# Moving three waits and one load in a single-core adaLN block with attention and a mixture of experts

## The reference

```python
h = _layernorm(x) * (1 + ca) + sa
normed = h * rsqrt(mean(h * h) + EPS)
q, k, v = heads(normed @ W_qkv.T + b_qkv)
scores = where(causal_mask, -inf, q @ k.T)
attn = softmax(scores, axis=-2)                 # over the queries
x = x + ga * ((attn @ v) @ W_o.T + b_o)
h2 = _layernorm(x) * (1 + cb) + sb
score = softmax(h2 @ Wg + bg); idx = argmax(score); gate = max(score)
pos = (cumsum(onehot) - 1) at idx               # rank of the token in its expert
keep = pos < 256
y = relu(buf[e] @ W1[e] + b1[e]) @ W2[e] + b2[e]   # buf: kept rows, by expert and rank
x = x + gb * where(keep, y[idx, pos] * gate, 0)
```

## Time and profile before

| what | value |
|---|---|
| median of 3 runs | 1332.78 us (1331.36 to 1332.94) |
| profiled execution, its own time | 1330.97 us |
| its span, first to last instruction | 1329.2 us |
| mean granted clock of TensorE, share of full | 0.954 |
| PE busy | 1212.8 us (91%) |
| DVE, ACT, POOL busy | 857.6, 602.1, 342.0 us |
| chain that ended last | PE 76%, issue 9%, ACT 6%, DVE 6%, DMA 1%, POOL 1% |

### The profile page before, as it was taken

The page is one execution under the profiler, slowest core; times in us unless marked ns, Lnnn a source line. Parts: engine busy times, 40 slices in busy tenths (PEclk is TensorE's granted clock), DMA queues, the critical chain, the costliest instruction groups (busy, mean ns, idle before and its releaser), DMA issues.

```text
span 1329.2 us, 23812 instructions
## 1 busy us (share of the span) xinstructions
PE 1212.8 (91%) x7522; PEld 859.4 (65%) x7522; DVE 857.6 (65%) x2172; ACT 602.1 (45%) x1419; POOL 342.0 (26%) x529
## 2 busy tenths in 40 slices
PE   5788888889999999999999999998998848999995
PEld 2555555556666666666666666665665747999994
DVE  6566666666676666676666666665665455777773
ACT  2455455555555555555555555554554022333320
POOL 4221212212332323233233222233433150111111
PEclk7899889999999999999999999998998868999998
DMA  4521202011121222121221212213435823767640
GB/s 147 189 89 48 104 24 104 34 36 66 60 76 62 84 69 75 56 71 61 71 77 56 72 62 89 82 51 122 149 131 191 283 88 136 260 202 248 205 150 18
DMA packets 100237, 139.58 MB, mean 105 GB/s; under 512 B 9916, under 2 KB 71486, under 8 KB 100032
## 3 DMA queue, kind: packets, MB, share of 16 engines
q1 hardware_dynamic: 91600, 113.55, 26.0%
q10 hardware_dynamic: 4464, 16.25, 3.1%
q0 software_dynamic: 4096, 8.82, 1.8%
HBM read 94.50 MB, written 48.00 MB: 107 GB/s over the span
## 4 chain that ended last, share of the span: by engine, by line
PE 76%; issue 9%; ACT 6%; DVE 6%; DMA 1%; POOL 1%; DVEq 0%; SPq 0%; ACTq 0%; POOLq 0%
PE SC L797 18%; PE Z L817 17%; PE Z L976 8%; PE SC L949 7%; PE XA L853 7%; ACT E L1017 5%; PE XA L769 5%; PE XB L769 4%; PE XA L779 3%; PE XB L779 3%; PE SC L734 1%; PE XB L839 1%; DVE V L1307 1%; DMA xp<-in_x 1%; DVE nm L1319 1%
## 5 line engine op out<-in xcount | busy, mean ns | idle before, releaser
L1017 ACT ACTIVATE E<-SC,nm 128x512 f32<-128x512 f32 (+7 forms) x512 | 375.0, 740 | 431.2 <-DVE nm L1319 431.2
L1319 DVE CUSTOM_DVE_ANT_0 SC<-SC,mask 128x512 f32<-128x512 f32 (+7 forms) x512 | 375.8, 785 | 225.7 <-PE SC L797 225.4
L797 PE MATMUL SC<-XQ,XK 64*128 64x512 f32 (+3 forms) x2304 | 271.2, 368 | 49.2 <-ACT E L1017 47.2
L797 PEld LDWEIGHTS SC<-XQ,XK 64*128 64x128 f32 x2304 | 187.8, 191 | 149.4 <-issue 132.0
L817 PE MATMUL Z<-E,vs 128*64 128x512 f32 (+3 forms) x1536 | 270.8, 495 | 0.3 <-DVE vs L1295 0.3
L817 PEld LDWEIGHTS Z<-E,vs 128*64 128x64 f32 x1536 | 100.0, 137 | 137.8 <-issue 127.8
L976 PE MATMUL Z<-W,hh 128*128 128x256 f32 x512 | 113.2, 379 | 2.3 <-issue 2.3
L976 PEld LDWEIGHTS Z<-W,hh 128*128 128x128 f32 x512 | 96.0, 190 | 15.1 <-issue 2.7
L1017 ACT ACTIVATION_READ_ACCUMULATOR E<-SC,nm 128x1 f32 x512 | 101.4, 198 | 0.0
L853 PE MATMUL XA<-woT,zt 128*128 128x256 f32 x384 | 91.4, 392 | 5.1 <-DMA xp<-in_x 5.1
L853 PEld LDWEIGHTS XA<-woT,zt 128*128 128x128 f32 x384 | 72.5, 194 | 22.9 <-issue 13.5
(11 more groups left out here) (247 smaller groups left out, 1982.1 us busy)
## 6 DMA issues: line engine op xcount, KB each, us to landing
W<-in_w SPq DMA_DIRECT2D x32, 1024.0 KB, 8.2
z_s<-zs ACTq DMA_DIRECT2D x31, 512.0 KB, 2.6
zt<-z_s SPq DMA_DIRECT2D x24, 512.0 KB, 3.8
W<-in_wqk SPq DMA_DIRECT2D x33, 257.0 KB, 2.7
slots_s<-zt SPq DMA_DIRECT2D x16, 520.0 KB, 4.0
xb<-slots_s SPq DMA_DIRECT2D x16, 520.0 KB, 3.8
Wv<-in_wv SPq DMA_DIRECT2D x17, 256.0 KB, 2.6
xln<-in_x SPq DMA_DIRECT2D x24, 128.0 KB, 2.4
```

The source lines that it names most:

```text
L797: last = pe.matmul(SC[h][:, at:at + z - a], XK[rows, ap, kp, lo:lo + P], XQ[rows, ap, qp, a:z], start=(t == 0), stop=(t == 2))
L1017: act.activation(E[:, h, EOFF[kb]:EOFF[kb + 1]], SC[h][:, at:at + S - lo], ACT.Exp, bias=nm[:, h, kb:kb + 1], scale=-1.0, accum_out=rs[:, ...
L1319: dve.tensor_tensor_reduce(SC[h][:, at:at + S - lo], SC[h][:, at:at + S - lo], mask[:, 0:S - lo], 1.0, BIG, ALU.add, ALU.min, nm[:, h, kb: ...
```

## The change

The loads of the first lot's rows move from the end of the step before to the middle of the step that sends them, after the loads of weights and ahead of the x1 and h2 stores; the first of them waits for two more tiles' stores. PE's wait for the columns of hT ahead of q stays only in the first step of a batch; for that the first couple of steps of batch 2 is written out instead of being part of a loop. The waits for the banks ahead of the tail's `project_out(1)` are gone or stand at `turn(0)` (the others stood a second time ahead of `lot_ranks(1, XA)`, and stay there). The tail's tiles are routed in two groups of four instead of groups of two, four and two.

```diff
-SETTLED = [(0, 2), (2, 4), (6, 2)]
+SETTLED = [(0, 4), (4, 4)]
@@ SEGS
-    (2, 0, 3, (0, 1), ("late", "att", "proj", "ln", "post")),
+    (2, 0, 1, (0, 1), ("late", "att", "proj", "ln", "post")),
+    (2, 1, 3, (0, 1), ("late", "att", "proj", "ln", "post")),
@@ SP, step, after the load of xln
+                n = round_at(st, RANK + 1)
+                if n is not None:
+                    if n == 0:
+                        sp.wait_ge(auxa_full, st.n("auxa"))
+                        sp.wait_ge(auxb_full, st.n("auxb"))
+                        for k in range(2):
+                            sp.wait_ge(post_out[k], 48 * (TPB + 1) + ONE)
+                    else:
+                        sp.wait_ge(lead_sent, 16 * LEAD * n)
+                    for k in range(2):
+                        first = LEAD * n + LEAD // 2 * k
+                        sp.dma_start(lead[k][:, :, 0:2 * D], ...).then_inc(lead_in, 16)
                 if st.has("post"):
                     sp.wait_ge(s["x1"], st.of("x1", 1))
@@ SP, step, after the store of h2
-                n = round_at(st, RANK)
-                if n is not None:
...
-                        sp.dma_start(lead[k][:, :, 0:2 * D], ...).then_inc(lead_in, 16)
@@ PE, project
                     if kind == "q" and half == 0:
                         pe.wait_ge(s["wsplit"], st.of("wsplit", 1))
-                        pe.wait_ge(auxa_free, st.n("auxa"))
+                        if isinstance(st.j, int) and st.i == 0:
+                            pe.wait_ge(auxa_free, st.n("auxa"))
@@ PE, tail
-            pe.wait_ge(auxa_free, TOTAL["auxa"])
-            pe.wait_ge(auxb_free, TOTAL["auxb"])
-            for h in range(2):
-                pe.wait_ge(exp_done[h], TOTAL["expd"])
-            pe.wait_ge(s["zevac"], TOTAL["zevac"])
             def turn(n):
                 u0, size = GROUPS[n]
+                if n == 0:
+                    pe.wait_ge(s["zevac"], TOTAL["zevac"])
                 pe.wait_ge(tail_h2, n + 1)
@@ PE, tail, order
             gate(1)
-            ranks(0)
             turn(2)
             gate(2)
             turn(3)
+            ranks(0)
             gate(3)
             ranks(1)
-            ranks(2)
@@ ACT, tail, order
             turned(1)
-            sums(0)
             turned(2)
             turned(3)
+            sums(0)
             sums(1)
-            sums(2)
@@ DVE, tail, order
             norm_tail(2)
-            route_tail(0)
             norm_tail(3)
             take_logits(1)
             take_logits(2)
+            route_tail(0)
+            take_logits(3)
             route_tail(1)
-            take_logits(3)
-            route_tail(2)
```

More of the change, by code:

```diff
@@ L598, in step @@
                     sp.dma_start(xln[:, 1 - st.pp, :], x_d[(st.b + 1) * TPB + st.i + 1]).then_inc(xln_in[1 - st.pp], 16)
+                n = round_at(st, RANK + 1)
[9 more added lines that the diff above has]
+                        first = LEAD * n + LEAD // 2 * k
+                        sp.dma_start(lead[k][:, :, 0:2 * D], xh_s[first:first + LEAD // 2].rearrange("t p d -> p t d")).then_inc(lead_in, 16)
                 if st.has("post"):
```

## The result

The changed kernel takes 1313.73 us (median of 5 runs, 1311.11 to 1314.31) against 1331.93 (5 runs, 1330.95 to 1332.94): ratio 0.987, 95% interval 0.986 to 0.988, or 17.3 us less. Forecast were 1315.4 us and 17.4 us. The profiled execution took 1314.31 us, the longest of the five; its span is 1312.6 us, the granted clock 0.959.

The account below looks back on a forecast made before the run. The prediction took a step to be bound by PE, and the tail by a chain through PE, DVE and POOL with no engine full. 7.1 + 1.2 + 9.1 = 17.4 us less gave 1315.4 us, range 1310.5 to 1320.5.

Parts of the forecast that it names:

- Part 1: Loads of rows, steps 27 and 28: with zt, xp and W ahead of the wait for scatters, 7.1 us less.
- Part 3: Tail: earlier project_out(1), regrouped routing and eight unbroken scatters end it 9.1 us earlier.
- The spare 0.5 us: Tail, power of norm_tail(2): DVE ready at 1060.6, POOL at 1061.1, so POOL sets the pace.
- The rival of a falling clock: Tail: clock falls in the new 1.5 us wait, project_out(2) takes 2.2 us more; 1317.1 us, chance 0.18.
- Late load: Step 28's load, or W, collides with something unseen; half of the 7.1 us returns: 1319 us, chance 0.08.
- held tail: Tail: POOL's eight scatters start no earlier, say because of weight loads; the 9.1 us vanish: 1324.5 us, chance 0.06.
- slower: Steps 28 to 30: SP held until scatters land, delaying x1, h2 and next zt; 1335.5 us, chance 0.03.
- more than forecast: q wins its full 2.5 us and the tail runs smoother: 1312.5 us, chance 0.10.
- Part 2: Wait ahead of q: six waits go at 0.2 us each, 1.2 us less, between 0 and 2.5.
- half remain: they begin batches, or lie in batch 0 where hTl comes in time: Waits for hTl ahead of q: of twelve, six go (i = 2, 4, 6 of batches 1 and 2).
- The experts behind are bound by PE and keep their length: Expert stage behind the tail: no change in its time entered the sum.
- The rule weighed: Tail, lot_scatter(1) beside line 1452: port blocking could cost 0.86 us, sum 0.9 us smaller; row showed 0.2, left out.

## Why the prediction was right

**Part 1** came out by its own steps: 7.2 us of 7.1, alone and with the rest, with zt 0.5 us behind the store and 10 us of slack ahead of x1 (9 were reckoned). The mechanism is shown; that the size fits to 0.1 us is luck of the trace that was read, for by the six traces with the old order it is 5.2 to 7.8. **Part 3** too: `norm_tail(1)` starts 7.2 us earlier against the last step, routing ends at 1065.82, which is 1076.4 on the time of before (its last step began 10.61 us later) against 1076.0 forecast, the last scatter 1086.6 against 1085.8. The tail gave 8.4 us of 9.1. The spare 0.5 us by which POOL was to set the pace was gone: PE's new wait made DVE late as well, and the two came to both powers together. The parts are nearly separate, 6.8 for the waits and 2.0 for the grouping make 8.4 together, and the grouping alone is worth little, as said. The rival of a falling clock did not come: the new wait was 2.2 us, not 1.5, because POOL's sums took 2.63 us instead of 2.31, and `project_out(2)` still took 6.9 us, at 1.00. Late load, held tail and slower did not come either. Of "more than forecast" q's part came, the smoother tail did not.

**Part 2** was mis-sized by a wrong count. "half remain: they begin batches, or lie in batch 0 where hTl comes in time" is the step that failed: nine of twelve went, three of them in batch 0, and only three remain. Two of these three are worth 0.4 us, or up to 2.3 where the clock did not fall; the third is not measured.

**"The experts behind are bound by PE and keep their length"** is the second step that failed: they were 2.4 us longer in the profiled execution, 0.5 in the next. The two groups of four leave PE standing still about 2 us longer ahead of them, and the lower clock then lasts longer into the first expert: in the profiled executions to 11.3 us behind the first load of slots, before to 9.6. Why the last expert is slow in some executions stays open. That the sum is closer than its terms is luck: in the profiled execution they were 2.4 us ahead of step 27 (1.2 forecast), 7.0 for the late steps (7.1), 1.2 of chance in step 31, 8.4 for the tail (9.1) and 2.4 lost by the experts (0).

**The rule weighed** was priced by a misread row, and the loss came beside another instruction. The Trainium skill (SBUF — State Buffer, Who interferes with whom) has the second comer blocked for the whole instruction, where DVE runs in a mode that takes both port pairs. The 0.86 us of the earlier trace rows for line 1452 are two instructions of 0.41 each. The scatter at 1079.12 began 0.17 us behind the first of them, so the 0.19 us that it lost are most of the 0.24 that were left of that one, and not a fifth of a block: this row agrees with the rule, whose price here is some 0.4 us and not 0.9.

In the changed kernel line 1452 (now 1448) had ended when `lot_scatter(1)` began. The row at 1052.26 is 1.56 us instead of 1.05, so 0.5 us: it began 0.06 us behind line 1450, a tensor_tensor, of which that sentence of the page does not speak, and what it lost is nearly the rest of that line's 0.69 us. It cost the tail little or nothing, for DVE was not ready for the last power before POOL was. Before, the scatter at the same place began 0.04 us behind that instruction and took 1.05, and the instruction 0.76: there DVE was held a little instead.

```profile
1069.91 0.76 DVE L1454 TENSOR_TENSOR th<-th,modB 128x512 f32<-128x512 f32 x1
1069.95 1.05 POOL L1783 DMA_INDIRECT slots_s<-xb,slot_u  x1 [0.81 <-POOL xb L1779]
```

What decides between the two is not settled by these rows.

## What to carry to other kernels

In one queue, put a wait for something slow behind the issues that the next stage needs, not ahead of them, and reckon the slack of what then stands behind it: that forecast held. When waits go, count them row by row, with the place of each, and not by a mean. And look past the stage that gets shorter: where PE idles longer there, the next stage can run longer at the lower clock, and work of no use in the idle time can be worth as much as a better order (0.9845 of the time before against 0.9842 here).

## What the hardware showed unexpectedly

PE's standing still ahead of the experts (13.3 us) left the granted clock at 0.5, the lower of its two levels, for their first matmuls. 24 useless float32 matmuls in that gap had it at 1.00 there and bought some 2.9 us (intervals overlap; the expert stage is 2 to 4 us shorter than in the two profiles of the changed kernel); 36 bought nothing as they ran over by 3.7.

A stretch at the lower clock in the first batches stands in some executions of one kernel and not in others: 673.9 and 672.1 us for the same steps in the two profiles of the changed kernel. For edits of 1 to 2 us that is as large as the effect.

The issue of an indirect DMA took 1.56 us beside a DVE tensor_tensor with both inputs in SBUF, in all of the five kernels where the two met as in the changed kernel (the changed one twice), and 1.05 where they met as before.
